# The second feed-forward of a gated four-layer block: dense experts replaced by rows sorted by expert through DRAM, token attention and third feed-forward interleaved with it

## The chip, the core and the metric

The kernel runs on one core of one Trainium2 chip. It is one launch with TensorE (PE), VectorE (DVE), ScalarE (ACT), GpSimd (POOL) and the sync engine (SP), each with its own instruction stream, which meet only through semaphores. The metric is the device time of one execution, in microseconds.

## The reference, cut to what matters

`x` is 32 sequences of 128 tokens with 128 features, 4096 tokens in all. Four layers follow each other, each an attention and then a feed-forward, both added to `x` with a gate `tanh(g)`:

```python
x = x + tanh(g_xattn[0]) * attention(layernorm(x), ctx)        # 16 heads of 8
x = x + tanh(g_ffn[0])   * fp8_linear(layernorm(x))
x = x + tanh(g_xattn[1]) * attention(layernorm(x), ctx)        # "second attention"
x = x + tanh(g_ffn[1])   * moe(layernorm(x))                   # "second feed-forward": the change
x = x + tanh(g_xattn[2]) * token_attention(layernorm(x), ctx)  # 16 x 16 among the heads of a token
x = x + tanh(g_ffn[2])   * relu_ffn(layernorm(x))              # "third feed-forward"
x = x + tanh(g_xattn[3]) * attention(layernorm(x), ctx)        # "last attention"
x = x + tanh(g_ffn[3])   * moe3(x)                             # "last feed-forward"

def moe(xf):                       # 8 experts, 352 hidden units, 128 features
    topw, topi = top_k(softmax(xf @ w_router.T), 2); topw /= sum(topw)
    combine = scatter of topw to topi          # tokens x 8, two entries of 8 are not zero
    down = (silu(xf @ w_gate[e].T) * (xf @ w_up[e].T)) @ w_down[e].T     for each expert e
    return sum over e of combine[:, e] * down[e]
```

Each token needs two of the eight experts; the other six have weight zero.

## The kernel before

`x` stays in SBUF for the whole kernel, 32 tiles of 128 tokens. A *group* is four tiles (`TG = 4`, `GT = 512` columns), so there are eight groups (`NG = 8`). A tile is numbered `n`, a group `gr` or `g`. Each engine has a function for each stage and runs them in the order written out by hand; nothing is scheduled by a planner. The helper `walk` writes out the first two and the last two groups and puts the four between them into a loop.

**The second feed-forward** (`feed_forward1`, `feed_forward1_and_tokens`) is dense. The 8 x 352 hidden units are cut into 22 chunks of 128 (`NC1 = 22`), six of which hold units of two experts (`MIXED`). For each group and each chunk `c` PE makes a gate product (L1199, 128x512 columns) and an up product (L1205), ACT takes the gate through SiLU (`work`, L845), DVE multiplies them (`hide`, L1664, and for a mixed chunk L1672), and two chunks later PE adds the down products of the four tiles into a bank (L1181, four matmuls, each recorded as two). The share of a token in an expert is multiplied onto the input of the up product (`xw`, L1654), so all experts of a token sum in the same bank. The shares go through DRAM (`share_rows`) to be spread over partitions. Routing (`top2`, L1589 to L1630) of the next group is done beside it, in pieces between `hide` calls. All matrices are in fp32.

**Token attention** (the third one) works on one tile at a time and leaves PE out. POOL multiplies queries and keys (`products`, L647, four instructions), DVE sums and shifts them (`score`, L1727 to L1737), ACT takes the exponential (`token_exp`, L829), DVE normalises (`probabilities`, L1741 to L1747), POOL multiplies with the values (`weighted`, L660, four instructions), DVE sums and adds to `x` (`combine`, L1753 and L1758). There is one buffer of each kind: `products` of a tile waits for `score` of the one before, `weighted` waits for `probabilities` of its tile and for `combine` of the one before. The tiles of group `g - 1` run between the chunks of group `g`, by the tables `SCORE_SLOTS`, `EXP_SLOTS` and `COMBINE_SLOTS`. Before a group's tiles, `norm_stats` (L1351, L1356), `inv_std` on POOL (L506, L508) and `norm` (L1374) make its normalised input.

**The third feed-forward** (`feed_forward2`) is a stage of its own behind them: for each group norm, transpose (L1122), copy (L819), four up products (L1225), four ReLUs (L867), down products (L1233), add (L1779, L1784). The last four tiles of token attention run inside it, one in each of its first four groups. The first steps of the last attention (`take_xnT`, `project`, `split`) stand there too.

**The last attention** needs rows of queries and keys at other partitions; SP moves them with 18 small DMAs for each group (`spread`, L377 and L381).

## Time and profile before

| | |
|---|---|
| times of three runs | 1754.88, 1756.35, 1757.84 us, median 1756.35 |
| profiled execution, own time | 1759.78 us |
| its span, first to last instruction | 1757.7 us |
| mean granted clock of TensorE | 0.923 of full speed |

Busy time counts instructions on an engine. PE busy is modelled from pipelined matmuls, so it says where the work lies and not how near the peak it is. The stages follow each other in time; a share over the whole span is an average over stages with different limits. The clock stands at one of two levels, 1.2 or 2.4 GHz, given as 0.5 or 1.0 of full speed, and a stretch with 0.75 is a mean of both.

### The profile page before, as it was taken

To read this page: it belongs to the slowest core of one execution; us is meant where nothing else is said; L and a number is where in the kernel's file an instruction comes from. 1 tells how busy PE (TensorE), PEld (TensorE's weight loads), DVE (VectorE), ACT (ScalarE), POOL (GpSimd) and SP (SyncE) were. 2 spreads that over 40 slices of the span, in tenths; PEclk is the share of its full clock that TensorE was granted. 3 is DMA by queue.
4 is the path that set the end of the run, shared out by engine and by line. 5 is a ranking of instruction groups with operands and counts; after the bars stand their busy time and mean duration, and the time that the engine had idled before them with its cause. 6 is when DMAs were issued, how large, how long until landed. Compare 5 with 4: busy or idle time off the path is not lost. (4 is left out here: it accounts for less than half of the span.)

```text
span 1757.7 us, 32824 instructions
## 1 busy us (share of the span) xinstructions
PE 1407.4 (80%) x10456; PEld 897.4 (51%) x10456; DVE 1318.4 (75%) x3282; ACT 727.7 (41%) x1306; POOL 690.7 (39%) x718
## 2 busy tenths in 40 slices
PE   3888883489989998988988989565589897878787
PEld 1555552256666565554545545333266664455454
DVE  5768776676767569889788897877467564899898
ACT  1455552156656324334333343232166564333333
POOL 0223211023341024445354454454024431687786
PEclk9999996599999999999999999877699998899899
DMA  8455530364532221020220211000554450000000
GB/s 187 66 81 69 70 49 1 44 159 66 73 49 37 91 84 68 29 79 22 80 68 24 84 35 64 12 1 1 101 69 68 60 69 5 1 13 1 13 12 12
DMA packets 73205, 92.98 MB, mean 53 GB/s; under 512 B 7984, under 2 KB 59952, under 8 KB 70448
## 3 DMA queue, kind: packets, MB, share of 16 engines
q1 hardware_dynamic: 73072, 91.36, 26.6%
q8 instruction: 65, 1.06, 0.3%
q14 instruction: 68, 0.56, 0.1%
HBM read 51.35 MB, written 2.23 MB: 30 GB/s over the span
## 5 line engine op out<-in xcount | busy, mean ns | idle before, releaser
L1400 DVE TENSOR_REDUCE neg_max<-bank 128x4 f32<-128x512 f32 x384 | 252.7, 686 | 149.5 <-PE bank L966 147.7
L764 ACT ACTIVATE probs<-bank 128x512 f32<-128x512 f32 x384 | 212.3, 596 | 169.8 <-PE bank L993 169.0
L1181 PEld LDWEIGHTS bank<-room,area 128*128 128x128 f32 x1408 | 188.6, 195 | 83.9 <-issue 80.2
L845 ACT ACTIVATE work<-bank 128x512 f32<-128x512 f32 x176 | 105.1, 597 | 292.1 <-PE bank L1199 246.7
L964 PE MATMUL bank<-mask_b,ident_b 128*128 128x512 bf16 x384 | 155.9, 406 | 76.0 <-DMA k_rows<-area 50.5
L506 POOL TENSOR_SCALAR rstd_a<-meanvar 128x4 f32<-128x4 f32 x64 | 15.9, 249 | 457.9 <-DVE meanvar L1356 371.4
L660 POOL TENSOR_TENSOR prod<-mask_i,work 128x128 f32<-128x128 f32 (+3 forms) x128 | 133.7, 1075 | 157.9 <-DVE mask_i L1747 157.9
L1181 PE MATMUL bank<-room,area 128*128 128x128 f32 x1408 | 189.5, 279 | 0.0
L1199 PE MATMUL bank<-xT,room 128*128 128x512 f32 x352 | 183.0, 602 | 0.0
L1664 DVE TENSOR_TENSOR area<-work,bank 128x512 f32<-128x512 f32 x176 | 119.2, 682 | 56.7 <-PE bank L1205 50.5
L1205 PE MATMUL bank<-area,room 128*128 128x512 f32 x256 | 134.7, 608 | 28.4 <-DVE area L1664 16.8
L966 PE MATMUL bank<-k_rows,q_rows 96*128 96x256 bf16 x768 | 156.6, 287 | 0.0
L757 ACT ACTIVATE q_rows<-bank 32x512 bf16<-32x512 bf16 x192 | 103.0, 582 | 120.6 <-PE bank L976 116.9
L983 PE MATMUL bank<-ident_b,mask_b 128*128 128x512 bf16 x384 | 134.9, 393 | 3.0 <-ACT probs L764 1.8
L993 PE MATMUL bank<-q_rows,k_rows 128*128 128x128 bf16 x1536 | 135.9, 222 | 0.0
L647 POOL TENSOR_TENSOR probs<-h,work 128x128 f32<-128x128 f32 (+3 forms) x128 | 120.0, 967 | 23.4 <-DVE probs L1727 13.0
L993 PEld LDWEIGHTS bank<-q_rows,k_rows 128*128 128x128 bf16 x1536 | 112.5, 100 | 27.8 <-issue 2.2
L1007 PE MATMUL bank<-probs,v_aug 128*32 128x128 f32 x3072 | 112.9, 288 | 0.8
L515 POOL CAST area<-area 128x1024 bf16<-128x1024 f32 x19 | 19.7, 1036 | 227.6 <-DMA k_rows<-area 170.2
L966 PEld LDWEIGHTS bank<-k_rows,q_rows 96*128 96x128 bf16 x768 | 78.6, 102 | 54.0 <-issue 11.2
L585 POOL TENSOR_TENSOR probs<-probs,work 128x512 f32<-128x512 f32 x64 | 82.5, 1289 | 50.1 <-DVE probs L1854 50.1
L1205 PEld LDWEIGHTS bank<-area,room 128*128 128x128 f32 x256 | 46.7, 191 | 99.8 <-issue 42.4
(182 smaller groups left out, 2789.2 us busy)
## 6 DMA issues: line engine op xcount, KB each, us to landing
q_rows<-area SPq DMA_DIRECT2D x144, 128.0 KB
k_rows<-area SPq DMA_DIRECT2D x288, 64.0 KB
q_rows<-share_rows SPq DMA_DIRECT2D x16, 1024.0 KB, 4.6
ctxT<-ctx_t SPq DMA_DIRECT2D x24, 256.0 KB, 7.7
ctxT<-share_rows SPq DMA_DIRECT2D x32, 128.0 KB, 3.7
ctxT<-share_rows SPq DMA_DIRECT2D x16, 192.0 KB, 3.6
xnT<-share_rows SPq DMA_DIRECT2D x16, 192.0 KB, 3.5
mask_i<-mask SPq DMA_DIRECT2D x8, 256.0 KB, 8.5
```

The lines of the kernel that those rows point to most:

```text
L647: ins = pool.tensor_tensor(prod[:, at:at + 4 * nj * DH].rearrange("p (i j d) -> p i j d", i=4, j=nj), q[:, 4 * i:4 * i + 4, :].unsqueeze(2 ...
L660: ins = pool.tensor_tensor(prod2[:, at:at + 4 * nj * DH].rearrange("p (i d j) -> p i d j", i=4, d=DH), tok_p[:, 4 * i:4 * i + 4, 0:nj].uns ...
L764: act.activation(probs[j].rearrange("p a b -> p (a b)"), T_BANK[j % 2][:], ACT.Exp).then_inc(exp_done, 1)
L964: pe.matmul(dst[:], ident_b[:], bcast(mask(b, t), 4), start=True, stop=False)
L966: mm = pe.matmul(dst[:, 256 * i:256 * i + 256], q_rows[b][SCORE_ROWS, 2 * j + i, tok], k_rows[b][SCORE_ROWS, :, 2 * j + i, tok], start=Fal ...
L983: pe.matmul(T_BANK[j % 2][:], mask(b, t), bcast(ident_b[:], 4), start=True, stop=False)
L993: mm = pe.matmul(dst[:, i * P:(i + 1) * P], k_rows[b][:, j % 2, hp, tok], q_rows[b][:, hp, tok], start=False, stop=i == 3)
L1181: mm = pe.matmul(dst[:, t * P:(t + 1) * P], hidden1[(c + 2 * b) % 4][:, t * P:(t + 1) * P], wd[:, c, :], start=False, stop=c == NC1 - 1 an ...
L1199: pe.matmul(S_BANK[c % 2][:], wg[:, P * c:P * (c + 1)], xT[b][:], start=True, stop=True).then_inc(gate_filled, 1)
L1205: pe.matmul(T_BANK[c % 2][:], wu[:, P * c:P * (c + 1)], xT[b][:] if mixed else xw[e % 2], start=True, stop=True).then_inc(up_filled, 1)
L1400: dve.tensor_reduce(neg_max[:, 4 * j:4 * j + 4], S_BANK[j % 2][:].rearrange("p (h k) -> p h k", h=4), AX.X, ALU.max, negate=True).then_inc ...
L1664: ins = dve.tensor_tensor(h, work[c % 2][:], T_BANK[c % 2][:], ALU.mult)
```

## The change

**Rows are sorted.** The dense second feed-forward goes away. The 4096 tokens are cut into four chunks of 1024 (`NCH = 4`, `TC = 8` tiles). For each chunk, DVE normalises the eight tiles (`route_norm`), PE makes the router logits, DVE picks the two experts (`choose`), PE counts for each of the 2048 (token, expert) pairs how many stand before it (`ranks`, 17 matmuls with a triangle and with ones), and DVE turns that into a row number in a DRAM table (`put`), where each expert begins at a multiple of 128 rows. POOL then writes the rows there with indirect DMAs, 16 for each chunk, 128 rows of 512 bytes each (`scatter`). A chunk's region has 24 blocks of 128 rows (`NBLK = 24`), whatever the routing; four blocks are a *quad*, so there are 6 quads for each chunk and 24 in all (`NK`), 96 blocks (`NB`). Rows that no token takes are zero: SP clears the whole table, 6.3 MB, at the start of the second stage (`clear_rows`).

**Blocks go through one expert each.** SP loads a quad from DRAM, PE transposes it, and for each block PE makes gate and up products (352 columns each), ACT and DVE make the hidden rows, PE transposes them (3 matmuls), ACT copies them, PE makes the down product (3 matmuls), ACT copies the quad's result and SP stores it to the same rows. Which expert's weights a block takes is read at run time: PE loads one number for each quad from SBUF into a register and takes its parts as an offset into `room`.

**Results come back.** POOL gathers each tile's two rows with two indirect DMAs (`gather`, 64 in all), and DVE adds them to `x` with their weights (`add_taken`, two instructions for each tile).

**Token attention starts late and the third feed-forward is woven in.** Tile `n` of token attention stands in quad `n + 9` (`FIRST_STEP = 9`), so tiles 0 to 14 run beside quads 9 to 23 and tiles 15 to 31 behind them. The eight groups of the third feed-forward and the start of the last attention are placed between tiles 15 to 31 by the tables `FFN2_STATS`, `FFN2_NORM`, `FFN2_ADD`, `NEXT_STATS` and `NEXT_NORM`. The last group of the third feed-forward comes after the last tile. Stage `feed_forward2` is then empty on POOL, ACT and DVE.

Parts of the diff, cut to what the text speaks of:

```diff
-NC1 = E * I1 // P
...
+QUAD = 4
+NQ = 6
+NBLK = QUAD * NQ
+REGION = NBLK * P
+NK = NCH * NQ
+NB = QUAD * NK
+FIRST_STEP = 9
...
+            def clear_rows():
+                sp.wait_ge(zeros_made, 1)
+                for c in range(NCH):
+                    sp.dma_start(moe_rows[c * REGION:(c + 1) * REGION].rearrange("(p i a) d -> p i (a d)", p=P, a=4),
+                                 bcast(zeros, REGION // (4 * P))).then_inc(zeroed, 16)
...
+            def scatter(c):
+                pool.wait_ge(placed, c + 1)
+                if c == 0:
+                    pool.wait_ge(zeroed, 16 * NCH)
+                waits_apart(pool)
+                for o in range(2 * TC):
+                    t = o // 2
+                    pool.indirect_dma_start(
+                        moe_rows, bass.IndirectOffsetOnAxis(place_i[:, c, o:o + 1].bitcast(mybir.dt.uint32), 0),
+                        rows_of(c, t // TG)[:, t % TG, :], None).then_inc(scattered[c], 16)
...
             def feed_forward1_and_tokens():
...
+                route_std(2)
+                scatter(1)
+                route_std(3)
+                scatter(2)
+                scatter(3)
+                gather(0, range(TG))
+                token_std(0)
+                products(0)
+                at = 3 * NG
+                for n in range(NT):
+                    g, t = divmod(n, TG)
+                    if n + 1 < NT:
+                        products(n + 1)
+                    for events in (FFN2_STATS, NEXT_STATS):
+                        if n in events:
+                            at += 1
+                            inv_std(at)
+                    weighted(n)
+                    if g + 1 < NG:
+                        if t < 2:
+                            gather(g + 1, range(2 * t, 2 * t + 2))
+                        if t == 2:
+                            token_std(g + 1)
...
+                def experts(k):
...
+                    four = pe.value_load(expert_i[0:1, c, q:q + 1], min_val=0, max_val=E ** QUAD - 1)
+                    for j in range(QUAD):
+                        weights_at[k, j] = pe.snap(((four >> 3 * j) & (E - 1)) * EXPERT_W)
...
+                for k in range(NK):
+                    n = k - FIRST_STEP
+                    hide(QUAD * k)
...
+                    if n >= 0:
                         score(n)
+                    hide(QUAD * k + 1)
+                    if k in (1, 3, 5):
+                        put(k // 2 + 1)
+                    if k in (1, 3):
+                        route_norm(k + 3)
+                    if n >= 0:
+                        combine_last(n)
...
+                    hide(QUAD * k + 2)
...
+                    if n >= 0:
+                        between(n)
                         probabilities(n)
+                    hide(QUAD * k + 3)
+                    if k in (0, 2, 4):
+                        choose(k // 2 + 1)
...
+                for n in range(NK - FIRST_STEP, NT):
+                    score(n)
+                    combine_last(n)
+                    between(n)
+                    if n in FFN2_ADD:
+                        ffn2_add(FFN2_ADD[n])
+                    if n in FFN2_NORM:
+                        ffn2_norm(FFN2_NORM[n])
```

The first lines are constants, `clear_rows` is SP's, `scatter` and the loop with `gather` POOL's, `experts` PE's, and the last two loops are DVE's. `route_norm` of the last chunk waits for the scatters of the second one (`scattered[1]`), whose room it takes. `between(n)` is `add_taken` and `token_stats` of the next group at its third tile, and `token_norm` at its fourth.

On POOL, in the middle of a group of token attention, the program of before reads as follows (`prod<-mask_i` is `weighted`, `probs<-h` is `products`):

```order
L660 TENSOR_TENSOR prod<-mask_i,work 128x384
L660 TENSOR_TENSOR prod<-mask_i,work 128x512
L647 TENSOR_TENSOR probs<-h,work 128x128
L647 TENSOR_TENSOR probs<-h,work 128x256
L647 TENSOR_TENSOR probs<-h,work 128x384
L647 TENSOR_TENSOR probs<-h,work 128x512
L660 TENSOR_TENSOR prod<-mask_i,work 128x128
```

The same place in the changed program, from the end of `products(1)` on (L745 is `weighted`, L594 `gather`, L731 `products`):

```order
L745 TENSOR_TENSOR prod<-mask_i,v_aug 128x128
L745 TENSOR_TENSOR prod<-mask_i,v_aug 128x256
L745 TENSOR_TENSOR prod<-mask_i,v_aug 128x384
L745 TENSOR_TENSOR prod<-mask_i,v_aug 128x512
L594 DMA mask_b<-moe_rows,m2b 128x128 x4
L731 TENSOR_TENSOR probs<-h,v_aug 128x128
L731 TENSOR_TENSOR probs<-h,v_aug 128x256
L731 TENSOR_TENSOR probs<-h,v_aug 128x384
L731 TENSOR_TENSOR probs<-h,v_aug 128x512
```

Four indirect DMAs have come in between `weighted` of a tile and `products` of the tile after the next; they stand behind the first two tiles of each group.

On DVE, between the scores of one tile and the scores of the next, the program of before has chunks and routing among the token work (L1664 is `hide` of 512 columns, L1611 to L1617 the routing of the next group):

```order
L1737 TENSOR_TENSOR probs<-probs,mask_i 128x256
L1664 TENSOR_TENSOR area<-work,bank 128x512
L1611 TENSOR_TENSOR route<-route 128x32
L1613 TENSOR_TENSOR route<-route,rows 128x32
L1615 TENSOR_REDUCE route<-route 128x4
L1617 TENSOR_TENSOR route<-rows,route 128x32
L1664 TENSOR_TENSOR area<-work,bank 128x512
```

In the changed program a quad with the third tile of a group reads (L1913 is `hide` of 352 columns, L2043 and L2048 `combine`, L1882 `add_taken`, L1891 and L1894 `token_stats`, L2031 to L2037 `probabilities`):

```order
L2027 TENSOR_TENSOR probs<-probs,mask_i 128x256
L1913 TENSOR_TENSOR area<-work,bank 128x352
L2043 TENSOR_REDUCE mask_i<-prod 128x32 x4
L2048 SCALAR_TENSOR_TENSOR x<-mask_i,gates,x 128x128
L1913 TENSOR_TENSOR area<-work,bank 128x352
L1882 SCALAR_TENSOR_TENSOR x<-ctxT,m2b,x 128x128 x8
L1891 BN_STATS m2b<-x 128x6 x4
L1894 BN_AGGR m2b<-m2b 128x2 x4
L2031 TENSOR_REDUCE mask_i<-probs 128x16
L2033 RECIPROCAL mask_i<-mask_i 128x16
L2037 TENSOR_TENSOR mask_i<-probs,mask_i 128x256
L1913 TENSOR_TENSOR area<-work,bank 128x352 x2
```

Eight additions and eight statistics instructions now stand ahead of `probabilities` in that quad, and there is one `hide` of 352 columns in each gap where one or two of 512 columns stood.

On PE a quad of the changed program begins with a load of the expert numbers, and each product that takes weights sets its address first (`ISA`, `REGISTER_ALU`), where the loop of before read from fixed places:

```order
L1299 TENSOR_LOAD m2b
L1299 ISA x2
L1310 REGISTER_ALU
L1310 ISA
L1310 MATMUL bank<-room,area 128x352
L1314 ISA
L1314 MATMUL bank<-room,area 128x352
L1322 MATMUL bank<-ident,area 128x128 x2
L1322 MATMUL bank<-ident,area 96x128
L1331 ISA
L1331 MATMUL bank<-room,area 128x128
```

For a block it is now two products of 352 columns, three transposes and three down products, against two of 512 columns and four down products for a chunk of before.

## Rows read from the trace of the kernel before

**Rows 1.** Windows: stretch, busy us by engine, PE clock, DMA share, GB/s.

```profile
576.60:1127.20 550.60, 492.71 (x2213) 303.26 (x2211) 453.77 (x1006) 195.02 (x282) 242.60 (x253) 0.98 0.17 56
1127.20:1258.30 131.10, 63.56 (x257) 35.76 (x256) 82.82 (x217) 33.32 (x51) 52.23 (x60) 0.72 0.14 23
```

**Rows 2.** Timeline of PE, first matmul of groups 0 and 1: start, us, what.

```profile
582.45 0.38 PE L1179 MATMUL bank<-ident_b,zeros_b 128*128 128x512 bf16 x1
...
641.52 0.38 PE L1179 MATMUL bank<-ident_b,zeros_b 128*128 128x512 bf16 x1
```

**Rows 3.** Timeline of PE, one chunk of the dense stage.

```profile
583.56 1.02 PE L1199 MATMUL bank<-xT,room 128*128 128x512 f32 x2
584.42 1.02 PE L1205 MATMUL bank<-area,room 128*128 128x512 f32 x2
585.28 1.05 PE L1181 MATMUL bank<-room,area 128*128 128x128 f32 x8
```

**Rows 4.** Timeline of DVE, one tile with one group of feed-forward three.

```profile
1166.07 0.69 DVE L1779 TENSOR_TENSOR o<-bank,b_q 128x512 f16<-128x512 f32 x1 [2.92 <-PE bank L1233]
...
1167.54 1.66 DVE L1753 TENSOR_REDUCE mask_i<-prod 128x32 f32<-128x128 f32 x4
...
1169.50 0.41 DVE L1741 TENSOR_REDUCE mask_i<-probs 128x16 f32<-128x256 f32 x1
...
1170.58 0.86 DVE L1351 BATCH_NORM_STATS2 stats<-x 128x6 f32<-128x128 f32 x4
...
1171.84 1.63 DVE L1727 TENSOR_REDUCE probs<-probs 128x16 f32<-128x128 f32 x4
...
1175.07 3.71 DVE L1374 TENSOR_SCALAR xn<-x,meanvar,rstd 128x128 f32<-128x128 f32 x4
1181.69 0.69 DVE L1779 TENSOR_TENSOR o<-bank,b_q 128x512 f16<-128x512 f32 x1 [2.92 <-PE bank L1233]
```

**Rows 5.** Lines of POOL: names, shapes, count | busy us, mean ns | idle.

```profile
L660 POOL TENSOR_TENSOR prod<-mask_i,work 128x128 f32<-128x128 f32 (+3 forms) x128 | 133.7, 1075 | 157.9 <-DVE mask_i L1747 157.9
L647 POOL TENSOR_TENSOR probs<-h,work 128x128 f32<-128x128 f32 (+3 forms) x128 | 120.0, 967 | 23.4 <-DVE probs L1727 13.0 <-DVE h L1374 10.3
...
L508 POOL TENSOR_TENSOR rstd<-rstd_a,minus_half 128x4 f32<-128x4 f32 x64 | 68.6, 1072 | 5.3
...
L517 POOL TENSOR_TENSOR area<-area 128x1024 f32<-128x1024 f32 x19 | 40.4, 2129 | 1.5
```

**Rows 6.** Timeline of DVE in the dense stage, an undisturbed norm.

```profile
790.17 1.11 DVE L1374 TENSOR_SCALAR h<-x,meanvar,rstd 128x128 f32 x4 [0.33 <-POOL rstd L508]
```

**Rows 7.** Source view of one DVE line: ns min/median/max, first and last start.

```profile
L1732 DVE TENSOR_TENSOR probs<-probs,rows x32: 424/1168/1189, 656.0 to 1189.1; 128x256 f32<-128x256 f32 x32
```

**Rows 8.** Timeline of SP's queue, the last attention's small DMAs.

```profile
1238.06 3.85 SPq L377 DMA_DIRECT2D q_rows<-area  x6
1241.96 8.53 SPq L381 DMA_DIRECT2D k_rows<-area  x12
```

**Rows 9.** Timeline of PE, two waiting stretches.

```profile
307.78 2.08 PE L942 MATMUL bank<-ctxT,wa 128*128 128x512 f32 x2 [0.78 <-ACT area L743]
...
1258.36 0.58 PE L964 MATMUL bank<-mask_b,ident_b 128*128 128x512 bf16 x1 [13.10 <-DMA k_rows<-area]
```

**Rows 10.** DMA issues: out<-in, queue, count, KB each, median us to landing.

```profile
work<-ctx_in SPq DMA_DIRECT2D x8, 256.0 KB, 2.8
```

**Rows 11.** Timeline of SP's queue, end of the first stage.

```profile
238.93 1.35 SPq L363 DMA_DIRECT2D ctxT<-ctx_t  x2
```

**Rows 12.** Timeline of DVE, one routing operation.

```profile
563.54 0.19 DVE L1615 TENSOR_REDUCE route<-route 128x4 f32<-128x32 f32 x1
```

**Rows 13.** Lines of DVE, the addition of a tile to x.

```profile
L1758 DVE SCALAR_TENSOR_TENSOR x<-mask_i,gates,x 128x128 f32<-128x128 f32 (+1 forms) x32 | 11.3, 352 | 1.1
```

**Rows 14.** Timeline of DVE, last but one group of feed-forward three.

```profile
1223.14 0.86 DVE L1351 BATCH_NORM_STATS2 stats<-x 128x6 f32<-128x128 f32 x4
...
1233.47 0.75 DVE L1784 SCALAR_TENSOR_TENSOR x<-o,gates,x 128x512 f32<-128x512 f16 x1
```

More of the change, by code:

```diff
@@ L384, in attention @@
                 if start:
+                    if a == 2:
+                        sp.wait_ge(x_mixed, TG * EARLY)
                     load_ctx(0, 0)
@@ L1444, in attention @@
                 xc = NT * BLOCK[a]
+                if part is not None:
+                    if part < 3:
+                        split(0, part)
+                    else:
+                        take_v(0, 0)
+                    return
                 if start:
@@ new lines, in route_norm @@
+            def route_norm(g):
+                c, half = divmod(g, 2)
+                if half == 0:
+                    dve.wait_ge(r_rstd_ready, c + 1)
+                    if c == 1:
+                        dve.wait_ge(t_filled, 4 * (2 * NT - TG))
+                    if c == 3:
+                        dve.wait_ge(scattered[1], 16 * 2 * TC)
+                for t in range(TG):
+                    n = TG * half + t
+                    ins = dve.tensor_scalar(rows_of(c, half)[:, t, :], tile(TG * g + t), r_meanvar[:, n, 0:1],
+                                            r_rstd[:, n:n + 1], ALU.subtract, ALU.mult)
+                ins.then_inc(rows_ready, 1)
```

1171 lines of the change are left out of this document (636 added, 535 removed).

## The prediction, made before the changed kernel ran

> **What bounds the kernel now.** I read the windows by stage first, then the timelines inside the two stages that the change touches, then the waits between POOL and DVE. The dense stage runs from 576.6 to 1127.2 us and the third feed-forward to 1258.3 us [rows 1]; the first products of the last attention start at 1258.36 [rows 9]. These 681.8 us are what the change rebuilds. The rest is the same program, apart from the routing of the first chunk, which now stands in the tail of the second attention, and the clearing DMAs.
>
> In the dense stage PE is busy for 493 of 551 us and DVE for 454 [rows 1]. Group 0, without token attention beside it, takes 59.1 us [rows 2]; the seven others take (550.6 - 59.1) / 7 = 70.2 us each. So PE alone would need about 59 us for a group, and 11 us come from the coupling with DVE's token work. In the third feed-forward no engine is full: PE 64 of 131 us, DVE 83, and the clock stands at 0.72 [rows 1]. There the chain sets the pace: one group and one tile every 1181.69 - 1166.07 = 15.6 us [rows 4], and at the end PE waits 13.1 us for the small DMAs of the last attention [rows 9], which SP takes 3.85 + 8.53 = 12.4 us to issue [rows 8].
>
> **What is removed.** PE's dense work: 176 chunks, each two products of 0.86 us and eight passes of a down product [rows 3]. Group 0's 59.1 us over 22 chunks are 2.69 us for each, so eight passes take 0.97, 0.12 each. The mixed chunks' extra multiplications, the share loads and the stage of the third feed-forward go too. DVE's `hide` of 0.68 us at 512 columns is 0.47 us at 352.
>
> **What PE does now.** A block takes 2 x 0.59 (352 columns), 3 + 1 transposes of one pass and 6 passes of the down product: 1.18 + 10 x 0.12 = 2.4 us, a quad 9.5 us. The register load at the head of a quad has no row. It lies between nothing, where PE's engine still has matmuls queued, and 2.8 us, the landing time of a plain load [rows 10]; I take 0.5, near the lower end, since a few queued passes cover it. That gives 10.0 us a quad, 240 us for all 24, against about 493.
>
> **What POOL does now.** Token attention costs it 120.0 / 32 = 3.75 us for `products` and 133.7 / 32 = 4.18 us for `weighted`, for each tile [rows 5]. New are 128 indirect DMAs. No row shows one. The lower bound is SP's issue of a small DMA, 12.4 / 18 = 0.69 us [rows 8]; the upper one is POOL's longest instruction, 2.13 us [rows 5]. I take 1.07 us, that of L508, POOL's dearest instruction for its size (four elements), since the cost of an indirect DMA is also not in the bytes. The Trainium skill, page "DMA: Bandwidth & Descriptors", section "Latency and other measured facts", gives about 1 us to the first byte of a DMA that GpSimd describes in software; by that the sum below would be some 6 us lower. No run here shows it yet.
>
> **The new stretch, in five terms.**
>
> *Start, 22 us.* `put(0)` stands in the third tile of the second attention's last group: some 20 operations of 0.2 to 0.4 us [rows 12], 6 us, so with its successors the tail gets about 5 us longer. Then come 16 scatters, 17 us, the landing and the load of the first quad, 2.8 us each [rows 10], and a transpose and a copy. Part of this lies under the last two tiles, so PE's first block starts about 17 us after its last attention matmul where it started at once.
>
> *Quads 0 to 8, 115 us.* 9 x 10.0 = 90. PE also transposes, ranks and routes three chunks: 24 transposes, 48 passes of router products, 51 short ranks, about 12 us. On DVE `choose` (3 us) and `put` (6 us) stand between `hide` calls; PE is at most two blocks ahead, about 4 us, so they cost 1 and 3 us each, three times, 12 us. In quad 3 `route_norm` of the last chunk waits for the scatters of the second one, started in quad 1 and 17 us long: 1 us.
>
> *Quads 9 to 23, 207 us.* PE's 10.0 us are no longer the longest. From the end of `score(n)`: two `hide`s 1.0, `combine` 2.0, `probabilities` 1.1 [rows 4], 0.3 for hand-offs, `weighted` 4.2, four gathers 4.3, and only then `products` of the next tile but one: 12.9 us at the first two positions of a group. At the third, `add_taken` (8 x 0.35 = 2.8 [rows 13] alone; 4.8 beside POOL) and the statistics (1.3) come ahead of `probabilities`, and POOL's square root (1.3) behind: 16.0. At the fourth the norm must be ready before `products`: 1.0 + 2.0 + 2.4 + 3.75 + 4.2 = 13.4. I take a norm at 2.4 us, between 1.1 alone [rows 6] and 3.7 beside POOL [rows 4]; the same holds for additions, whose median is 1168 ns and smallest 424 [rows 7]. The mean is 13.8 us, times 15 tiles.
>
> *Tiles 15 to 31, 252 us.* Without `hide`, but with add 1.5, norm 2.4 and statistics 1.3 of the third feed-forward [rows 4] ahead of `probabilities`: 17.1, 17.1, 20.2 and 15.2 us by position, 124 us for tiles 16 to 22. Tile 23 carries the split and the first values of the last attention, about 23 us; 15 and 24 to 27 take 13 to 16.5 us each, 70 together; the last four have no gathers and take 35.
>
> *Tail and clock, 20 us.* The last `combine` 2.0, then a group of the third feed-forward from its statistics to its addition, 1234.2 - 1223.1 = 11.1 us [rows 14], and 3 us to the first scores. The 13.1 us for small DMAs go: `spread` of the first group is issued some 100 us earlier. PE resumes at 1.2 GHz after a wait (a pair of 512 columns 2.08 us [rows 9] against 1.02 [rows 3]); 4 us for that.
>
> Sum: 22 + 115 + 207 + 252 + 20 = 616 us against 681.8, so 66 us less. The clearing writes 6.3 MB, the size of 24 loads of 256 KB. At 2.8 us each they would take 67 us; they start at 238.9 [rows 11] and PE wants the context at 307.8 [rows 9], so they are hidden, narrowly by this bound and well if they overlap. Without that cover they would cost what they are late. SP's quad loads and stores stand three quads ahead of their use. The profiled execution's own 1759.8 us become 1694; it lies 3.4 us above the median of the three runs, so the median becomes **1690 us**.
>
> Of POOL's 128 indirect DMAs about 88 lie on the path: 16 at the start, 16 as soon as quad 3 waits for them, 56 of the gathers. So each 0.1 us of one is worth 9 us: 0.69 gives 1657, 2.13 gives 1783.
>
> **The rivals.**
>
> *POOL's path is cheap and DVE bounds (chance 0.22, about 1645 us).* With 0.7 us per indirect DMA and norms near 1.1 us, tiles behind 9 take DVE's own time: about 10.4 us in a quad, 12 behind. For it: additions at 424 ns occur too [rows 7]. Against it: POOL is busier than before, so they should be rarer.
>
> *Indirect DMAs are dear (0.10, about 1780 us, slower).* The place is POOL's queue, `gather` between `weighted(n)` and `products(n + 2)`. It decides from 1.07 + 66 / 88 = 1.8 us each: then the gain is gone. DVE instructions of the kind that held up a norm from 1.1 to 3.7 us beside POOL [rows 4, 6] would then hold up POOL's writing of descriptors. Against it: POOL's own four instructions stay near 1 us each beside the same DVE work [rows 5]. The Trainium skill, page "SBUF — State Buffer", section "SBUF: two separate sides", says that GpSimd cannot write descriptors while DVE is in a two-port mode, and that such a DMA of 620 ns then takes 3100; by that each of the 88 overlapped ones would cost 3.1 us, an estimate of 1870. Rows of before show the lock only from DVE's side.
>
> *PE drops to 1.2 GHz (0.05, about 1780 us, slower).* PE is at work 10.0 of 13.8 us. The dense stage at 493 of 551 stood at 0.98, the third feed-forward at 64 of 131 at 0.72 [rows 1]. At half clock a quad takes 19.5 us, 15 x 5.7 = 86 us more. Half of the quads would still leave a gain of 20, so it needs most of them.
>
> *The pace was the tokens' all along (0.05, about 1752 us, no change).* Then less PE work brings nothing. Against it: group 0 without tokens takes 59.1 us and a group with them only 11 more.
>
> *The forecast itself: 0.54*, between 1660 and 1725; 0.04 is left for waits that I do not see.
>
> **Numbers.** 1690 us. The range takes in the cheap case and stops short of the two dear ones: 1635 to 1760. A difference under 0.2% (3.5 us) can't be told from none here. Faster 0.81, same 0.04, slower 0.15.
>
> **What the profile would show.** Between the second and the last attention 616 us; PE's first block about 17 us after its last attention matmul; quads of 10 us until the first token products, near 14 with them; POOL the engine with the least idle time from the first gather to tile 27; each POOL DMA near 1.07 us; no wait for `k_rows` at the start of the last attention; clock above 0.9 while quads run. It is wrong if a POOL DMA takes 1.8 us or more, if PE is at 1.2 GHz in most quads, or if DVE has more idle time than POOL while tiles run.

## The result and the profile after

The changed kernel takes 1651.51 us (median of 4 runs, 1647.54 to 1654.87). The kernel before took 1756.85 beside it. The ratio is 0.9401, with a 95% interval of 0.9374 to 0.9428: That is 105 us less, where the forecast was 66 us less and 1690 us. The measured time lies in the stated range.

These are the windows of the rebuilt stretch in the changed kernel: start, quads without tokens, quads with them, tiles behind the quads (columns as in [rows 1]):

```profile
583.60:597.00 13.40, 2.54 (x12) 1.93 (x12) 0.62 (x2) 0.61 (x2) 7.28 (x10) 0.59 0.38 114
597.00:705.00 108.00, 97.65 (x613) 76.28 (x614) 50.59 (x198) 48.53 (x99) 59.23 (x62) 0.97 0.30 86
705.00:888.00 183.00, 152.62 (x811) 110.58 (x810) 146.29 (x332) 106.65 (x185) 138.54 (x151) 0.95 0.19 53
888.00:1131.00 243.00, 77.18 (x258) 38.32 (x257) 193.93 (x476) 40.28 (x69) 175.56 (x193) 0.62 0.12 27
```

Against [rows 1], PE's 556 busy us in the two old stages have become 330. The quads run at a clock of 0.95 to 0.97, the tiles behind them at 0.62. In the third window PE, DVE and POOL are busy for 153, 146 and 139 of 183 us, in the fourth DVE is the fullest with 194 of 243. No engine is full.

The timeline of PE in the changed kernel (start, us, what, idle time and releaser) gives the marks: the first load that PE waits for, the first block, quad 9 with a wait, and the last attention.

```profile
594.98 1.12 PE L1291 MATMUL bank<-ident,q_rows 128*128 128x128 f32 x4 [10.79 <-DMA q_rows<-moe_rows]
...
596.97 1.54 PE L1310 MATMUL bank<-room,area 128*128 x2
...
696.63 0.85 PE L1310 MATMUL bank<-room,area 128*128 x2
701.73 1.17 PE L1314 MATMUL bank<-room,area 128*128 x2 [4.24 <-DVE area L1913]
...
1147.65 1.07 PE L1385 MATMUL bank<-w_q,hq 128*128 128x128 fp8e4 x16 [0.78 <-ACT hq L960]
1150.35 1.16 PE L1034 MATMUL bank<-wa,ctxT 128*128 128x128 f32 x8 [1.64 <-DVE x L2011]
1151.35 0.38 PE L1051 MATMUL bank<-mask_b,ident_b 128*128 128x512 bf16 x1
```

The last attention's first scores stand at 1151.35 without a wait, where [rows 9] has 13.10 us for the small DMAs. The forecast counts from 576.6, the end of the second attention in the kernel before. From there it is 575 us, where 616 were forecast and the kernel before took 681.8. In the changed kernel's own trace the attention's last matmul ends at 584.1, and from there it is 567 us. The difference of 7.5 us is part of the first term. By terms:

| term | from | to | forecast | measured |
|---|---|---|---|---|
| start | 576.6 | 596.97 | 22 | 20 |
| quads 0 to 8 | 596.97 | 696.63 | 115 | 100 |
| quads 9 to 23 | 696.63 | 889 | 207 | 192 |
| tiles to the last `weighted` | 889 | 1132.4 | 252 | 243 |
| tail | 1132.4 | 1151.35 | 20 | 19 |

The mark 889 is the start of the last block's up product; its down products end at 892.3.

The tokens are read from POOL's timeline. This is one part of a group in the changed kernel, from `weighted` of the first tile (L745) to `products` of the next group (L731):

```profile
767.47 3.87 POOL L745 TENSOR_TENSOR prod<-mask_i,v_aug 128x128 f32<-128x128 f32 x4 [1.74 <-DVE mask_i L2037]
...
776.39 3.31 POOL L731 TENSOR_TENSOR probs<-xnT,v_aug 128x128 f32<-128x128 f32 x4
780.07 3.89 POOL L745 TENSOR_TENSOR prod<-mask_i,v_aug 128x128 f32<-128x128 f32 x4 [0.36 <-DVE mask_i L2037]
784.11 0.98 POOL L594 DMA_INDIRECT ctxT<-moe_rows,m2b  x1 [0.16 <-issue]
785.40 0.95 POOL L594 DMA_INDIRECT ctxT<-moe_rows,m2b  x1 [0.30 <-issue]
786.66 0.94 POOL L594 DMA_INDIRECT ctxT<-moe_rows,m2b  x1 [0.30 <-issue]
787.90 0.94 POOL L594 DMA_INDIRECT ctxT<-moe_rows,m2b  x1 [0.30 <-issue]
788.86 3.30 POOL L731 TENSOR_TENSOR probs<-xnT,v_aug 128x128 f32<-128x128 f32 x4
796.73 3.88 POOL L745 TENSOR_TENSOR prod<-mask_i,v_aug 128x128 f32<-128x128 f32 x4 [4.57 <-DVE mask_i L2037]
800.59 0.40 POOL L563 TENSOR_SCALAR m2b<-m2b 128x4 f32<-128x4 f32 x1
801.07 1.05 POOL L565 TENSOR_TENSOR m2b<-m2b,minus_half 128x4 f32<-128x4 f32 x1
806.05 3.51 POOL L731 TENSOR_TENSOR probs<-h,v_aug 128x128 f32<-128x128 f32 x4 [3.93 <-DVE h L1901]
```

An indirect DMA takes 0.95 us of POOL, and 0.30 us pass before the next: 1.26 us each. Over all 128 of them in this kernel it stays between 0.94 and 1.30 us, whatever DVE does beside it. Behind the second and the third tile POOL waits for DVE, 4.57 and 3.93 us. DVE's timeline shows the first of these waits from the other side (L1882 is `add_taken`, L1901 the norm):

```profile
783.69 0.55 DVE L2022 TENSOR_TENSOR probs<-probs,rows 128x256 f32<-128x256 f32 x1
...
785.50 1.66 DVE L2043 TENSOR_REDUCE mask_i<-prod 128x32 f32<-128x128 f32 x4
...
790.41 3.87 DVE L1882 SCALAR_TENSOR_TENSOR x<-ctxT,m2b,x 128x128 f32<-128x128 f32 x8 [0.81 <-DMA ctxT<-moe_rows,m2b]
794.32 0.87 DVE L1891 BATCH_NORM_STATS2 m2b<-x 128x6 f32<-128x128 f32 x4
...
804.86 1.11 DVE L1901 TENSOR_SCALAR h<-x,m2b 128x128 f32<-128x128 f32 x4
```

`combine` (L2043) runs at 785.50, while POOL still issues gathers. The last gather goes out at 787.90 and DVE waits for its rows until 790.41.

The interval from one `weighted` to the next repeats group after group. Its four positions are named here by the tile that it starts from:

| from tile of its group | what lies in it | changed kernel, in quads | tiles 16 to 20 |
|---|---|---|---|
| first | four gathers, `products` | 12.6 | 16.0 |
| second | four gathers, landing, addition, statistics | 16.65 | 21.25 |
| third | deviations, norm, `products` | 12.5 to 12.9 | 15.2 |
| fourth | `combine`, probabilities | 9.27 | 10.8 |
| a group | | 51.2 | 63.3 |

The forecast had 55.2 and 69.6 for a group.

### The profile page after: what moved, and what is told of

The parts are those of the page before. It is cut to its first block and busy times, and to the rows that moved or that the text cites. A ratio compares the mean times of both kernels' runs of the same rounds, so it can differ in the third digit from the quotient of the medians.

```text
span 1647.2 us, 31338 instructions
## 1 busy us (share of the span) xinstructions
PE 1186.6 (72%) x9741; PEld 789.5 (48%) x9741; DVE 1185.9 (72%) x3134; ACT 699.4 (42%) x1333; POOL 790.9 (48%) x834
## 3 DMA queue, kind: packets, MB, share of 16 engines
q0 software_dynamic: 4096, 8.40, 1.7%
## 5 line engine op out<-in xcount | busy, mean ns | idle before, releaser
L606 POOL CAST area<-area 128x1024 bf16<-128x1024 f32 x36 | 37.3, 1036 | 219.8 <-DMA k_rows<-area 167.1
L1913 DVE TENSOR_TENSOR area<-work,bank 128x352 f32<-128x352 f32 x96 | 49.0, 516 | 81.6 <-PE bank L1314 71.6
L1209 PE MATMUL bank<-ident,xn 128*128 128x128 f32 x32 | 8.9, 433 | 123.3 <-DVE xn L1507 113.6
L1241 PEld LDWEIGHTS bank<-room,area 128*128 128x128 f32 x512 | 67.2, 199 | 44.8 <-issue 20.6
L1051 PEld LDWEIGHTS bank<-mask_b,ident_b 128*128 128x128 bf16 x384 | 37.8, 99 | 104.8 <-DVE neg_max L1533 36.6
L1314 PE MATMUL bank<-room,area 128*128 x192 | 76.7, 482 | 14.7 <-DVE area L1913 14.5
L1094 PEld LDWEIGHTS bank<-probs,v_aug 128*32 128x32 f32 x3072 | 85.7, 114 | 3.2 <-issue 1.6
L682 POOL TENSOR_TENSOR area<-probs,work 128x512 f32<-128x512 f32 x64 | 81.2, 1268 | 11.7 <-POOL probs L665 5.7
L1331 PE MATMUL bank<-room,area 128*128 (+1 forms) x576 | 85.4, 287 | 1.1
L1241 PE MATMUL bank<-room,area 128*128 128x128 f32 x512 | 73.0, 288 | 15.2 <-POOL area L682 15.2
```

Of the source, the lines that this page charges most:

```text
L682: pool.tensor_tensor(hidden[e % 2][:, 0, :], product[e % 2], work[2 + e % 2][:], ALU.mult).then_inc(hidden_ready, 1)
L1051: pe.matmul(dst[:], ident_b[:], bcast(mask(b, t), 4), start=True, stop=False)
L1094: mm = pe.matmul(O_BANK[32 * i:32 * i + 32, half * P:(half + 1) * P], v_aug[b][:].rearrange("p t h c -> p (t h c)")[:, at:at + 32], probs[ ...
L1241: mm = pe.matmul(dst[:, t * P:(t + 1) * P], h[:, t * P:(t + 1) * P], w, start=i == 0, stop=i == len(terms) - 1)
L1331: mm = pe.matmul(R_BANK[:, m * P:(m + 1) * P], hid_t[i % 3][0:n, j * P:(j + 1) * P], room[0:n, bass.ds(weights_at[k, m] + 2 * I1 + P * j, ...
```

## The experiments

All ten are variants of the changed kernel. Each time is a median beside the kernel before on the same chip, and the ratio is to that kernel. From run to run the early stages shift: in the eleven traces of the changed kernel and its variants the second attention's last matmul ends between 576.6 and 588.1 us. So a median can't place a difference of some 5 us, and I also compare within the traces. The *rebuilt stretch* runs from the end of that matmul to the last attention's first scores, 567.2 us in the changed kernel. The *token stretch* runs from the first `weighted` to the end of the last, 416.1 us in the changed kernel. There is one trace of each kernel. Against the changed kernel:

| variant | median, us | rebuilt stretch, us |
|---|---|---|
| one gather instead of two | -29.8 | -26.6 |
| every gather twice | +76.8 | +77.6 |
| a lighter down product | +1.1 | +0.6 |
| the third feed-forward apart | +62.8 | +68.2 |
| norm earlier | -12.2 | -6.6 |
| gathers spread, norm earlier | -13.7 | -17.2 |
| gathers spread only | -11.6 | -7.3 |
| addition ahead of `combine` | -12.2 | -13.9 |
| token work earlier | -18.7 | -17.1 |
| `probabilities` ahead of the third `hide` | -14.8 | -20.2 |

### One gather instead of two

```
-                    for k in range(2):
+                    for k in range(1):
...
-                dve.wait_ge(gathered[g], 16 * 2 * TG)
+                dve.wait_ge(gathered[g], 16 * TG)
...
-  dve.scalar_tensor_tensor(xt, taken(g, t, k), weight[...], ...)
+  dve.scalar_tensor_tensor(xt, taken(g, t, 0), weight[...], ...)
```

> Of the two rows that a token gathers only the first is fetched, and the addition takes it for both (so the second expert's share is wrong); 32 of the 64 gathers go, DVE's work stays. Theory A, the queue of POOL: in the changed kernel `weighted` starts 12.6 us apart behind the first tile of a group, 16.65 behind the second, 12.6 behind the third and 9.27 behind the fourth; the first two have four gathers at 1.26 us from one to the next. Two fewer make that 10.1 and 14.1, so 5.0 us a group, 35 us for seven groups, and 5 us at the first gathers: about 1611 us. Rival B, DVE's own work sets the pace and POOL's DMAs lie in its idle time: at most 10 us, 1641 or more. Rival C, PE sets the pace while quads run: only the tiles behind 15 gain, about 20 us, 1631.

Measured: 1621.76 us, ratio 0.9228 (0.9201 to 0.9255), so 30 us less instead of 40. The first products come 5 us earlier, as expected. In the quads the interval behind a second tile falls from 16.65 to between 14.9 and 15.3, where 14.1 was expected, and behind a first tile only from 12.6 to between 11.5 and 12.3, where 10.1 was expected. So POOL's queue is on the path, but of the 2.5 us taken from it only 0.4 to 1.8 come through before the next bound is met.

### Every gather twice

```
+                        pool.indirect_dma_start(
+                            spare[2 * t + k], None, moe_rows,
+                            bass.IndirectOffsetOnAxis(place_i[:, g // 2, o:o + 1]...)
+                        ).then_inc(gathered[g], 16)
```

> Each gather is issued twice, the second time into a tile that nothing reads: 64 more DMAs on POOL, nothing more on the other engines. Theory A: 64 x 1.26 = 81 us slower than the changed kernel, about 1732 us; the landing of the second row adds nothing beyond that. Rival B: POOL's idle time (4.6 us behind the second tile and up to 3.9 behind the third) takes most of it, so 20 to 40 us, 1670 to 1690. If an indirect DMA's cost were in the wait for its descriptors' room in the queue, doubled density would make one dearer than 1.26 us and the time would pass 1750.

Measured: 1728.26 us, ratio 0.9847 (0.9815 to 0.9879). That is 76.8 us for 64 more DMAs, 1.20 us each against the 1.26 of the timeline. In the rebuilt stretch it is 77.6 us, 1.21 each. Theory A holds in this direction and rival B is out. (The edit also makes POOL wait, before a group's gathers, for those of the group before, which landed long ago.) The trace shows the doubled gathers still 1.25 us apart, so a denser queue makes none dearer.

### A lighter down product

```
-                    for j, (_, n) in enumerate(UNITS):
+                    for j, (_, n) in enumerate(UNITS[0:1]):
```

> The down product of a block takes its first unit of 128 hidden values alone instead of three (so the product is incomplete): four of six passes go, 0.11 us each, 0.45 us a block, 43 us of PE in all. Theory A: PE sets the pace in quads 0 to 8 alone, 36 blocks, so 8 to 16 us less (1635 to 1644), and nothing from quad 9 on, where PE waits for `hide`, which waits in DVE's order behind the tokens. Rival C, PE sets the pace in all quads: 43 us less, 1609. Rival D, ACT or DVE sets it in the first quads already: nothing, 1651.

Measured: 1652.59 us, ratio 0.9407 (0.9377 to 0.9437): nothing, and 0.6 us in the rebuilt stretch, where Theory A expected 8 to 16 us less. Rival D's number came true, but not for its reason. Quads 6 and 7 do run faster, 7.9 us from one to the next instead of 9.4. Then PE stands in quad 9 (timeline of this kernel):

```profile
694.80 0.85 PE L1310 MATMUL bank<-room,area 128*128 x2 [0.29 <-issue]
704.51 1.54 PE L1314 MATMUL bank<-room,area 128*128 x2 [8.86 <-DVE area L1913]
```

It waits 8.86 us for a `hide` where the full product left a wait of 4.24. DVE's `hide` stands behind the first `score`, which waits for POOL's first `products`, and those come at the end of 64 scatters and 8 gathers. That chain is not POOL's alone: in the changed kernel the last chunk's scatters, from 666.12 on, waited 4.52 us for DVE's row numbers. So PE's saving in quads 0 to 8 is given back within one quad. From there on PE's spare time is larger still.

### The third feed-forward apart

```
+        def later(table):
+            return {n + 17 if n < 27 else n + 16: g for n, g in table.items()}
...
-                for n in range(NT):
+                for n in range(END):
```

The loops of DVE, ACT and POOL go on to 47, without token work from 32.

> The third feed-forward is taken out of tiles 15 to 31 and runs behind tile 31, in the order and with the spacing of its tables, on the same engines; all that is computed stays. Theory A: its pieces on DVE (statistics 1.3, norm 1.1, addition 1.5 us a group) and on POOL stand in the chain of the tiles, 4 to 5 us for each group of the third feed-forward, and ACT's and PE's part (some 10 us a group) runs beside it. Apart, the tiles drop from 63.3 to about 48 us a group, 16 tiles 190 us, and the third feed-forward takes 8 groups at 11 to 13 us: 263 us become about 290, so about 25 us slower, 1677. Rival: its pieces are hidden anyway and the tiles keep 60 us a group, so apart costs the whole 90 us, 1740.

Measured: 1714.34 us, ratio 0.9764 (0.9723 to 0.9805), 63 us slower than interleaved instead of 25. The tiles behind the quads fell to 47.5 us a group, as expected (12.29, 16.57, 10.79 and 7.85). The third feed-forward alone was the surprise (window from the last `weighted` to the last attention's first scores):

```profile
1083.10:1215.30 132.20, 77.18 (x256) 36.45 (x257) 42.94 (x149) 30.70 (x46) 12.69 (x21) 0.70 0.16 28
```

Eight groups, with the last attention's first steps among them, take 132 us, 16.5 each and not 11 to 13. No engine is full: with PE busy for 77 us, DVE for 43 and a clock of 0.70, the time lies in the hand-offs between them. Without the interleaving the change would still have gained 42 us.

### Deviations and norm earlier

```
                     if n + 1 < NT:
                         products(n + 1)
...
+                    if g + 1 < NG and t == 2:
+                        token_std(g + 1)
                     weighted(n)
...
                     score(n)
+                    norm_between(n)
                     combine_last(n)
```

> POOL computes the reciprocal deviations of the next group's tokens ahead of `weighted` of a group's third tile instead of behind it, and DVE's norm moves from behind `combine` to ahead of it, so that `products` of the next group finds its input ready. Nothing is added or left out. Theory A2 (each of the four positions in a group has a chain of its own that sets its length, POOL's DMAs at two of them, the norm at the third): `weighted` behind the third tile comes 9.9 us after the one before instead of 12.5, and the other three stay at 12.6, 16.65 and 9.27. Seven groups, 18 us less: about 1633 us. Rival B (DVE's total sets the pace): the order changes nothing, 1651. Rival E (what one position gives back the next takes, since PE's blocks must be served anyway, 9.4 us a quad): at most half, 1642.

Measured: 1639.35 us, ratio 0.9331 (0.9299 to 0.9363), 12 us less by the medians but only 6.6 in the rebuilt stretch, where the whole edit lies. Behind the third tile the interval falls from 12.5 to 9.4, where 9.9 was forecast. But behind the fourth it grows from 9.27 to between 10.4 and 11.3, and behind the second from 16.65 to 17.05. The token stretch is 7.1 us shorter (408.98 us). Rival E was right in the quads: one half to two thirds of the saving are given back.

### The gathers spread, with and without the earlier norm

```
+        GATHERS = {0: [(1, 0, 4)], 1: [(1, 4, 8)], 4: [(2, 0, 4)], 5: [(2, 4, 8)], ...
+                   **{4 * g - 7 + i: [(g, a, b)] for g in range(5, NG)
+                      for i, (a, b) in enumerate(((0, 4), (4, 6), (6, 7), (7, 8)))}}
...
+                    for g1, first, last in GATHERS.get(n, ()):
+                        gather_rows(g1, first, last)
```

> The last kernel, and the eight gathers of a group are spread over the four positions (4 behind the second tile, where POOL has 6 us to spare while DVE adds the group before, then 2, 1 and 1), from the fourth group on; the second and third group keep four and four. Theory A2: behind the second tile `weighted` no longer waits for four gathers (5.0 us) and their landing (2.4 us), only for `combine`, addition, statistics and probabilities: about 13.3 us instead of 16.65; behind the first 10 to 11.5 instead of 12.6; the other two 9.5 and 10.1. So 4.5 us a group for five groups, 22 us below the last kernel: about 1611 us. Rival B: no change from the last kernel.

> The gathers spread in the same way, with the deviations and the norm where the changed kernel has them. Theory A2: the same 4.5 us a group, so about 22 us below the changed kernel, 1629, less 1 to 2 us a group where the gathers stand ahead of the deviations behind the third tile (2.5 us on the norm's chain, five times): 1629 to 1642. Rival B: 1651.

Measured: 1637.85 us with the earlier norm, ratio 0.9321 (0.9282 to 0.9361), and 1639.92 without it, ratio 0.932 (0.9287 to 0.9353). So they are 13.7 and 11.6 us below the changed kernel instead of 40 and 22, and 17.2 and 7.3 in the rebuilt stretch. With the norm earlier, the interval behind tile 9, in which no gather is left, is 13.37 us, and 13.3 was forecast. But behind tile 13, with four gathers of a later group in it, the interval is 17.18 us, although their landing is no longer waited for. From the second group on the third and fourth positions take 11.4 to 12.8 us in the quads, where 9.5 and 10.1 were forecast.

The windows over the token stretch say where it went. They belong, in this order, to the changed kernel, one gather, norm earlier, spread with the norm earlier, and spread only. Columns are as above.

```profile
716.29:1132.40 416.11, 222.15 (x1029) 143.66 (x1027) 333.99 (x792) 140.43 (x243) 308.52 (x336) 0.76 0.15 39
```

```profile
710.02:1104.83 394.81, 219.68 (x1029) 140.93 (x1028) 341.65 (x792) 140.41 (x244) 282.04 (x308) 0.77 0.14 37
```

```profile
713.41:1122.39 408.98, 221.42 (x1027) 143.89 (x1026) 328.41 (x792) 140.53 (x243) 308.35 (x336) 0.75 0.16 40
```

```profile
716.63:1116.08 399.45, 221.25 (x1027) 143.58 (x1025) 356.68 (x792) 140.45 (x243) 308.50 (x336) 0.76 0.16 41
```

```profile
712.14:1120.93 408.79, 229.22 (x1029) 146.87 (x1028) 338.50 (x792) 140.41 (x244) 310.18 (x336) 0.75 0.16 40
```

DVE executes the same 792 instructions in all five. They take 334 us in the changed kernel and 357 when the gathers are spread and the norm is earlier, and POOL's stay at 308.5. So DVE is busy for 89% of the stretch instead of 80%, and the growth of 23 us is longer instructions. The timelines of DVE and then of POOL in the spread kernel show two (L2059 is the addition in `combine`, L738 `products`):

```profile
814.50 2.64 DVE L2059 SCALAR_TENSOR_TENSOR x<-mask_i,gates,x 128x128 f32<-128x128 f32 x1
...
852.27 2.53 DVE L2048 TENSOR_TENSOR mask_i<-probs,mask_i 128x256 f32<-128x256 f32 x1
854.72 0.94 DVE L1919 TENSOR_TENSOR area<-work,bank 128x352 f32<-128x352 f32 x2
```

```profile
813.67 3.31 POOL L738 TENSOR_TENSOR probs<-h,v_aug 128x128 f32<-128x128 f32 x4
...
851.20 3.31 POOL L738 TENSOR_TENSOR probs<-xnT,v_aug 128x128 f32<-128x128 f32 x4
```

The multiplication (L2048) has a median of 425 ns and the addition one of 407. Here they end 0.3 and 0.2 us after POOL's `products` do.

The sum over all instructions says the same. I compared each of DVE's in the token stretch with the shortest of its operation, tiles and shape in the eleven traces. In the changed kernel 70 are over 0.3 us longer than that, by 58 us together; in the spread kernel with the norm earlier 71 are, by 82 us. In the changed kernel 67 of the 70 end at a fixed distance behind the end of an instruction of POOL's arithmetic, and in the spread kernel 65 of the 71: 0.28 us for TENSOR_TENSOR, 0.16 for SCALAR_TENSOR_TENSOR, 0.08 for TENSOR_SCALAR, each to within some hundredths. So the growth is time held beside POOL's arithmetic. Most of it is in the addition of `combine`, 20 us instead of 3. In the kernel with one gather, where `products` also comes sooner behind `weighted`, it is 18. The reductions are not held: they keep their length in all 32 tiles of this kernel (L2042 0.36 to 0.42 us, L2036 0.42), and so does `hide`, which reads one operand from PSUM (two of them 0.94 us in the row above). The Trainium skill, page "SBUF — State Buffer", section "SBUF: two separate sides", speaks of a port that DVE and GpSimd share. The side of it seen here is that DVE's instruction is the one held, by POOL's arithmetic. The other side, GpSimd's descriptors held by DVE, shows in no run: an indirect DMA stays between 0.94 and 1.35 us in all of them. None of them tests it with a long instruction of DVE, though: one tile of a norm (TENSOR_SCALAR) takes 0.34 us.

### The addition ahead of `combine`

```
-                    if t == 2 and g + 1 < NG:
+                    if t == 2 and g + 1 < NG and early == (g >= 2):
...
                         norm_between(n)
+                        between(n, True)
```

> As the spread kernel with the norm moved, and from the fourth group on DVE adds the gathered rows and takes their statistics ahead of `combine` instead of behind it, under `weighted` of the second tile (the rows landed long before). Theory A2: the position behind the second tile becomes about 12 us instead of 13.3, five times: 5 us below the spread kernel, about 1606. Rival: `combine` is what POOL waits for there, and the addition ahead of it delays `weighted` by as much as it saves: the same as the spread kernel within 2 us.

Measured: 1639.3 us, ratio 0.933 (0.9297 to 0.9363), the same as the spread kernel. The rival holds: behind tile 9 the interval even grew from 13.37 to 14.73, behind tile 13 it fell from 17.18 to 13.93, and the token stretch as a whole is 2.1 us longer than the spread kernel's.

### The token work earlier, and `probabilities` ahead of the third `hide`

```
-                scatter(3)
+                scatter(3, 0, 8)
                 gather(0, range(2 * TG))
+                scatter(3, 8, 14)
                 token_std(0)
                 products(0)
+                scatter(3, 14, 16)
```

> On top of the spread kernel, the start of the token work on POOL is reordered: eight scatters of the last chunk, the eight gathers of the first group, six more scatters while DVE adds that group's rows, and the last two behind the first `products`. Nothing is added or left out. Theory A3 (from the lighter down product: the first token products wait for POOL's scatters and gathers, not for PE's quads): the first gather can start about 676 us into the span, when quad 5's rows are stored, instead of 686, so the token work starts some 9 us earlier and ends 7 to 9 us earlier: about 1630 us where the spread kernel had 1638. Rival F (quad 9, in which DVE's order puts the first `score`, is what sets the start): no change, 1638.

Measured: 1632.85 us, ratio 0.9299 (0.9268 to 0.9331). The first `products` start 115.65 us after the second attention's last matmul instead of 120.8 in the spread kernel, 5 us earlier. The first `weighted` is only 2.4 us earlier, and the last attention begins as late after the second as there: 550.15 and 550.0 us. So the traces give none of the 5 us that the medians differ by; these were taken on different chips, and the intervals of the ratios overlap. Rival F is closer. One reason is in the rows of this kernel, DVE first, then POOL:

```profile
705.32 3.49 DVE L2040 TENSOR_TENSOR probs<-probs,mask_i 128x256 f32<-128x256 f32 x1
```

```profile
705.23 3.29 POOL L738 TENSOR_TENSOR probs<-h,v_aug 128x128 f32<-128x128 f32 x4
```

A subtraction whose smallest time is 424 ns stood through the whole of `products(1)`.

The last kernel is this one with another order in quads at the first two positions:

```
+                    early = n >= 0 and n % TG in (0, 1)
+                    if early:
+                        probabilities(n)
                     hide(QUAD * k + 2)
```

> On top of that, at the first two positions of a group DVE does `probabilities` ahead of the third `hide` of the quad instead of behind it, for which it sometimes waits 0.6 to 2 us on PE or ACT. Theory A3 (DVE, with what it waits at the port it shares with POOL, sets the pace in the quads; it has only 0 to 1 us of idle time a tile left there): 0.5 us a tile over some 8 tiles, 4 us or nothing, 1626 to 1630. Rival G (the chain from `combine` over `probabilities` to `weighted` still sets it): 1.5 to 2.5 us at each of these positions, 8 of them, 12 to 20 us, 1612. If PE falls behind because two `hide`s now follow each other, it is slower than the kernel before it by up to 2 us a quad.

Measured: 1636.72 us, ratio 0.9321 (0.9287 to 0.9355). By the medians it can't be told from the kernel without it; in the rebuilt stretch it is 3.1 us shorter. In its trace the intervals behind tiles 0 and 1 are 0.9 us longer and the one behind tile 3 is 2.3 us shorter. Rival G is out.

The lowest median is that of the spread kernel with its norm and start moved, 1632.85 us. It beats both kernels: the upper end of its interval, 0.9331, is below the lower end of the changed kernel's, 0.9374. Among the variants that compute everything and keep the interleaving without doubled gathers, its lead is not clear of the intervals.

## Why the prediction came out as it did

**The mechanism was right.** PE's dense work was taken away, and the token chain between POOL and DVE became the bound. The third experiment takes some 43 us of matmuls away from the changed kernel and gains nothing, and the second adds work to POOL alone and pays nearly all of it. The number was less so: 66 us less were forecast and 105 measured, and all five terms were too large.

**Start, 22 us forecast, 20 measured.** The first block follows the last attention matmul after 13 us, not 17. The scatters are dearer than I took them (1.26 us apart, not 1.07), but the first stands at 570.38, thirteen us before the attention's end. The rest of the term is the mark in the other trace: the attention ends 7.5 us later than 576.6 here, where 5 were forecast. One trace can't tell this from the shift between runs; the mean of the eleven traces is 582.5, 5.7 us behind the kernel before.

**Quads 0 to 8, 115 forecast, 100 measured: mis-sized and partly misread.** Undisturbed quads take 9.4 us instead of 10.0 (681.32 to 690.73 between the transposes of two quads), 5 us in all; the register load, taken at 0.5 us, leaves the matmuls a gap of 0.30 to 0.45 us in quads 2, 4 and 6 and none in quads 7 and 8. Routing and its stalls take 15 us instead of 25. And the step let PE set this term, with the tokens ready when quad 9 comes. In fact the chain of DVE's row numbers and POOL's scatters and gathers ends later: the lighter product shows that PE's share there was worth nothing at the end.

**Quads 9 to 23, 207 forecast, 192 measured: the step that failed is the serial sum of a tile.** For each group 55.2 us were forecast and 51.2 measured. Two terms were too large, because I took durations held up beside POOL: the norm 2.4 us (measured 1.11 in the quads) and `add_taken` 4.8 (2.6 to 3.9 for the groups added in the quads). And the sum put two `hide`s and `combine`, 3 us, in series with four gathers, 4.3 us. They are on two engines and overlap, as the rows at 785.50 show. What works against that is the gathers' price (5.0 us for four instead of 4.3) and their landing, 2.5 us, which I had left out behind the second tile. Put in the order of the measured intervals, the forecast's terms give 12.9, 19.0, 14.7 and 8.6 us; measured were 12.6, 16.65, 12.5 to 12.9 and 9.27. The first of these came near by luck. Its 12.9 us were two `hide`s, `combine`, `probabilities`, `weighted` and four gathers in a row. What POOL's rows from 767.47 to 780.07 show is its own queue, almost without idle time: `weighted` 3.9, four gathers 5.0, and `products` 3.3, which the sum did not have there. DVE's chain ends there within 0.4 us of it.

**Tiles 15 to 31, 252 forecast, 243 measured.** A group takes 63.3 us instead of 69.6. That this is the same overlap is likely but not summed up by rows here. A lag gives part of it back: the tokens of quad 23 end 14 us behind the quad. Tail and clock, 20 forecast, came out at 19, and the small DMAs' wait is gone.

**The price of an indirect DMA.** The row that I chose as its model, 1.07 us, was 0.19 too small. By the slope that makes 17 us on 88 of them and would have made the forecast worse, so the terms above were too large by more than the total shows. The slope itself, 1 us for each DMA on the path, measured 1.20 upwards (64 more) and 0.93 downwards (32 fewer), 1.21 and 0.83 in the rebuilt stretch.

**The rivals.** Dear indirect DMAs: out, about 0.95 us each beside all of DVE's work here and never above 1.35. PE at 1.2 GHz in the quads: out, the clock is 0.95 to 0.97 there. Tokens as the old bound: out. POOL cheap and DVE the bound, at about 1645 us: its time came nearest, but not through its cause. DMAs were dear, norms near 1.1 us were right, and DVE still waits for POOL. Of the signs I named, one was wrong: POOL was to have the least idle time from the first gather to tile 27, and DVE is the busier of the two, 314 of 404.5 us against 293. Together with POOL's gaps of 0.30 us behind the DMAs the two are level. The recorded text also contradicts itself here: it calls the forecast wrong if DVE has more idle time than POOL, which is the same state that it expects. Clearing `moe_rows` cost nothing visible: at 306.54 us PE waits 0.78 us for ACT as in [rows 9], not for its context.

**Where the gain stands.** With the third feed-forward wholly behind the tiles the change gives 42 us of the 105; 63 come from laying it between them.

**Open.** The intervals of the spread kernel were not predicted by any sum that has the held time in it, so it is open how much of the forecast 40 us the holds cost: DVE's instructions grew by 23 us, and the runs do not show how much of that lies on the path. Nor was it tried to start the scatters of the last chunk earlier, which needs another place for its routing in DVE's order.

## What to carry to other kernels

Once the full engine was relieved here, what remained was a chain across two engines that are 74 and 80% busy. Sum such a chain as intervals between two starts of one instruction, position by position, and ask for each term whether the other engine works beside it; durations from a crowded stage were too long for the terms here, and a landing time of 2.5 us was left out. A saving on one position of a repeating chain is worth what the next position does not take back: of 3.1 us behind the third tile up to 2.0 were lost again behind the fourth, and of forty forecast for the earlier norm and the spread gathers fourteen to seventeen were left. Where the early part of a kernel shifts by ten us from run to run, compare the changed stretch within the traces and not the medians alone.

## What the runs showed of the hardware

An indirect DMA of 128 rows of 512 bytes costs POOL mostly 0.94 to 0.97 us (up to 1.35) and 0.30 us until the next, for scatters and gathers alike and also in rows of sixteen. In the changed kernel a scatter has landed 2.2 us after its issue in the median and a gather 2.5, the slowest 4.0 and 4.6.

DVE's instructions with two operands in SBUF are held beside POOL's multiplications: 2.53 and 3.49 us for ones of 0.42. So is the norm, a TENSOR_SCALAR, of which one took 3.50 us instead of 0.34 in the changed kernel. They end 0.08 to 0.28 us, fixed by their kind, behind the end of one of POOL's instructions, and beside `products` that is often the last of the four. Reductions and `hide`, with one operand in PSUM, were never held. So DVE's busy time is no measure of its work: the same 792 instructions took between 328 and 357 us in the five kernels whose token stretch is shown above.

A chain of small stages on an otherwise idle core cost much more here than its instructions: eight groups of the third feed-forward took 132 us with PE busy for 77 and DVE for 43. With them laid between the tiles, the whole kernel was 63 us shorter.
